# Two expert layers: chunks written out on three engines in place of hardware loops, with a constant expert in the first layer

## The reference

```python
# layer 0: 8 experts, top 2, each expert takes at most 512 rows
slot = where(offset < capacity, expert * capacity + offset, dropped)
h = gelu_tanh(xb[e] @ w1[e]);  y = h @ w2[e]          # xb: (8, 512, 256), w1: 256x1024, w2: 1024x256
out[src] += weight * y
# layer 1: 8 experts, top 2, no capacity
h = gelu(x @ W1[e] + b1[e]);  y = h @ W2[e] + b2[e];  out = sum_e weight[t, e] * y
```

## Time and profile before

| what | value |
|---|---|
| median of 3 runs | 2665.28 us (2664.3 to 2670.51) |
| span of the profiled execution | 2672.0 us |
| PE busy | 2419.7 us, 91% |
| DVE, ACT, POOL busy | 71%, 63%, 68% |
| mean granted clock of PE | 0.972 |
| chunks of layer 0 | about 1507 to 1721 us of the span |
| chunks of layer 1 | about 2340 to 2656 us of the span |

### The profile page before, as it was taken

The page is one execution under the profiler, slowest core; times in us unless marked ns, Lnnn a source line. Parts: engine busy times, 40 slices in busy tenths (PEclk is TensorE's granted clock), DMA queues, the critical chain, the costliest instruction groups (busy, mean ns, idle before and its releaser), DMA issues. The chain is left out here.

```text
span 2672.0 us, 46118 instructions
## 1 busy us (share of the span) xinstructions
PE 2419.7 (91%) x14931; PEld 1416.2 (53%) x15058; DVE 1908.5 (71%) x3499; ACT 1673.2 (63%) x2692; POOL 1804.4 (68%) x1581
## 2 busy tenths in 40 slices
PE   6999999999999999999997588879999999678886
PEld 3555555555555555555553467645444444467665
DVE  7878777787777877777775655468888898764332
ACT  4556756557665566656664555458888788576453
POOL 2677867777777777776768455436878789355553
PEclk9999999999999999999999799989999999699998
DMA  4000000000000000000000744430202020573223
GB/s 144 1 1 1 25 1 1 1 1 5 22 1 1 1 1 1 1 1 1 1 1 15 193 112 116 92 97 18 57 17 58 2 49 1 165 202 72 35 39 60
DMA packets 90917, 107.85 MB, mean 40 GB/s; under 512 B 18867, under 2 KB 80260, under 8 KB 90708
## 3 DMA queue, kind: packets, MB, share of 16 engines
q1 hardware_dynamic: 68500, 80.57, 10.1%
q0 software_dynamic: 21696, 24.98, 6.1%
q10 hardware_dynamic: 544, 0.00, 0.0%
HBM read 68.75 MB, written 25.88 MB: 35 GB/s over the span
## 5 line engine op out<-in xcount | busy, mean ns | idle before, releaser
L417 POOL TENSOR_TENSOR a_acc<-a_acc,a_pf 128x512 f32<-128x512 f32 (+1 forms) x480 | 650.9, 1356 | 312.4 <-ACT a_pf L574 290.7
L574 ACT ACTIVATE a_pf<-a_psS 128x1024 f32<-128x1024 f32 (+1 forms) x288 | 281.5, 977 | 306.1 <-PE a_psS L717 301.8
L869 DVE TENSOR_TENSOR a_pl<-a_pf,a_ph 128x512 f16<-128x512 f32 x448 | 438.2, 988 | 23.2 <-ACT a_ph L580 23.0
L2161 POOL TENSOR_TENSOR c_pl<-c_pf,c_ph 128x512 f16<-128x512 f32 x320 | 374.9, 1199 | 116.9 <-ACT c_ph L2260 116.5
L845 DVE TENSOR_REDUCE a_mx<-a_psA 128x1 f32<-128x512 f32 x504 | 335.3, 683 | 43.7 <-PE a_psA L652 39.6
L580 ACT ACTIVATE a_ph<-a_psS 128x1024 f16<-128x1024 f32 (+1 forms) x288 | 281.5, 977 | 0.0
L1417 POOL DMA_INDIRECT f_sums<-f_xn,f_sidx x78 | 140.5, 1801 | 208.1 <-DVE f_xn L1815 185.6
L1261 DVE TENSOR_TENSOR f_xn<-f_xn 128x256 f16<-128x256 f32 x312 | 130.5, 424 | 197.8 <-ACT f_xn L1230 175.3
L2493 DVE TENSOR_REDUCE c_wf<-c_psA 128x1 f32<-128x512 f32 x384 | 246.5, 681 | 20.1 <-PE c_psA L2332 19.9
L1148 PE MATMUL f_psH<-f_xh,f_w 128*128 128x256 f16 x624 | 173.4, 278 | 83.3 <-ACT f_xn L1230 68.2
L2253 ACT ACTIVATE c_pf<-c_psS 128x1024 f32<-128x1024 f32 x192 | 197.9, 1030 | 67.1 <-PE c_psS L2366 66.0
(11 more groups left out here) (364 smaller groups left out, 6382.0 us busy)
## 6 DMA issues: line engine op xcount, KB each, us to landing
f_stage<-in_L_ffn_w SPq DMA_DIRECT2D x16, 1024.0 KB
f_stage<-in_L_ffn_W SPq DMA_DIRECT2D x16, 1024.0 KB
c_kst<-c_khs SPq DMA_DIRECT2D x64, 100.1 KB, 2.2
a_cx<-in_ctx SPq DMA_DIRECT2D x4, 1536.0 KB
c_cx<-in_ctx SPq DMA_DIRECT2D x12, 512.0 KB, 4.0
f_sums<-X SPq DMA_DIRECT2D x2, 2048.0 KB, 13.2
f_xrow<-f_xn SPq DMA_DIRECT2D x8, 512.0 KB, 4.4
c_kst<-c_kls SPq DMA_DIRECT2D x32, 100.1 KB, 2.2
```

The source lines that it names most:

```text
L417: g.tensor_tensor(acc[0:k, p, :], acc[0:k, p, :], pf[0:k, q % RF, i, :], ALU.add).then_inc(s_acc, 1)
L574: act.activation(pf[0:r, q % RF, 0:k, :], psS[q % 2][0:r, 0:k, :], ACT.Exp, scale=SCALE).then_inc(s_pF, 1)
L869: v.tensor_tensor(pl[0:r, q % RP, i, :], pf[0:r, q % RF, i, :], ph[0:r, q % RP, i, :], ALU.subtract).then_inc(s_pL, 1)
L2161: g.tensor_tensor(pl[0:r, q % RP, i, :], pf[0:r, q % RF, i, :], ph[0:r, q % RP, i, :], ALU.subtract).then_inc(s_pG, 1)
```

## The change

PE, ACT and DVE run their main chunk loops of both layers as Python loops: every iteration is written out as code of its own, with constants where the register m stood. In layer 0 PE takes the chunk's expert from a Python expression ((n + i) * 8 // 16, at most 7) and no longer loads it from `table`, whose iota on POOL goes. In layer 1 PE and DVE still load the expert from `table`, now at a constant place. SP's loop over the experts and the loops of the branch for ties at the kernel's end stay.

```diff
@@ pe_chunk
-            e, e_next = (pe.value_load(experts_of[0:1, bass.ds(c + (0 if last else i), 1)], min_val=0, max_val=E - 1)
-                         for i in range(2))
+            if experts_of is None:
+                e, e_next = (min((n + i) * E // NC, E - 1) for i in range(2))
+            else:
+                e, e_next = (pe.value_load(experts_of[0:1, bass.ds(c + (0 if last else i), 1)], min_val=0, max_val=E - 1)
+                             for i in range(2))
@@ gpsimd
-            else:
-                const(g.iota(table[:, :], pattern=[[1, E], [0, NC // E]], base=0, channel_multiplier=0))
@@ scalar
-                with act.Fori(first_m, last_m) as m:
+                for m in range(first_m, last_m):
                     for p in range(2):
                         act_chunk(act, main, m, p, splits)
@@ tensor
-                with pe.Fori(first_m, last_m) as m:
+                for m in range(first_m, last_m):
                     for p in range(2):
-                        pe_chunk(pe, main, m, p, table, m * 2 + p, splits)
+                        pe_chunk(pe, main, m, p, table if layer else None, m * 2 + p, splits)
...
-                pe_chunk(pe, main, n // 2, n % 2, table, n, False, last=n == NC - 1)
+                pe_chunk(pe, main, n // 2, n % 2, table if layer else None, n, False, last=n == NC - 1)
@@ vector
-                with v.Fori(first_m, last_m) as m:
+                for m in range(first_m, last_m):
                     for p in range(2):
                         dve_chunk(v, main, m, p, take_rows(m, p), splits, prepare_main(m, p))
```

## The result

The changed kernel takes 2624.82 us (median of 4 runs, 2623.94 to 2625.78), the kernel before on the same chip 2664.79 (2663.84 to 2670.51): a ratio of 0.9845, 95% interval 0.9831 to 0.9859. The span of the profiled execution is 2623.2 us, so the two profiles differ by 48.8 us; that of before was of a run some 6 us over its median.

A forecast was written before the change was run, and what follows sets the result against it. PE, busy for 91% of the span, was taken to set the pace. Layer 0 10.3, layer 1 6 and wake-ups 2 made 18.3 us off 2672.0, so 2653.7, scaled by 0.9975 to 2647; range 2632 to 2661.

The forecast's parts named there:

- What bounds the kernel: Expert stages of both layers: PE sets the pace, some 16% idle, nearly all before L1148; idle removed shortens the span.
- Layer 0, PE: Boundaries between layer 0's chunks: loads, branch and computed addresses go, 13.2 us less 2.9 us waiting for DVE, 10.3 us gained.
- The second gap: PE idle before hidden 2 of a chunk, put down to two expert loads and the branch: 13.2 us in layer 0.
- Layer 1, PE: Layer 1's chunk boundaries: the two loads stay, only the branch goes, 0.6 us at ten edges: 6 us, bounds 3 and 7.
- The first gap: PE idle before hidden 0 or 1 of the next chunk, 18.8 us in layer 0, ascribed to gathers; change taken as zero.
- Wake-ups: ACT's 35 ns register operation at loop waits goes: 0.035 to 0.1 us at 33 or so waits, taken as 2 us.
- Instruction streaming: First rival: written-out chunks need about 29 instruction packets, whose fetches could stall PE 35 us, giving 2682; chance 5%.
- The second rival: The gap before hidden 2 is ACT's or reappears elsewhere; only branches and wake-ups count, 3 to 7 us, 2660; chance 13%.
- The third: Rival: PE, less idle, keeps its full clock, about 5 us, and the first gap shrinks by 5: 2636; chance 16%.

The follow-up runs named there:

- merged_early_load_b: Changed kernel with token weights gathered inside the row gathers and, in layer 1, one expert loaded a chunk ahead, on a late-signal chip: 2590.33 us, 0.9693.
- loops_l0_register: Kernel before, loops kept, layer 0's expert from the loop's register instead of the table: 2597.79 us, 0.9994; again on a late-signal chip (_b): 2650.86 us, 0.9950.
- pool_late_l1_b: Changed kernel with three unused additions on POOL before each chunk's gathers in layer 1, on a late-signal chip: 2629.33 us, 0.9870.
- pe_only: Changed kernel with the loops of ACT and DVE put back, PE alone written out with the constant expert: 2646.82 us, 0.9891.
- before_merged_gather_b: Kernel before with token weights gathered inside the row gathers, the two gathers of 32-byte rows gone, on a late-signal chip: 2607.54 us, 0.9741.
- before_again: Kernel before, unchanged, run again for its profile on a chip with late signals: 2676.04 us, 1.0001.
- after_third: Changed kernel, unchanged, on the first chip, where no signal is late: 2590.74 us, 0.9972 of the kernel before.

## Why the prediction was wrong

**What bounds the kernel: right.** PE's idle time before L1148 came off the end: 32.0 - 0.2 - 4.4 = 27.4 us in layer 0 and 13.2 - 1.0 = 12.2 in layer 1 make 39.6 of the 48.8 us between the two spans. Of the rest some 3 us are one chunk of before that ran 17.1 us long beside the stretch at 1.2 GHz; in the chunks of layer 1 after, the granted clock is 1.00. What remains, some 6 us, lies in gaps under 0.2 us and in the first chunks of layer 1, and I haven't split it.

**Layer 0, PE (10.3 us): right in kind and size.** The second gap, 13.2 us, is gone, 4.6 us before L1166 came up, released by DVE L1264 as foreseen, against the 2.9 in the sum. The 0.21 us a chunk is exact where no signal is late at that place (every chunk of merged_early_load_b); here DVE's take starts another 0.1 us late on output 7's signal. The reason given for the gap needs a correction: loads, with the queue emptied before them or with a branch, make it, and a branch without loads makes none (layer 0 of loops_l0_register and of loops_l0_register_b).

**Layer 1, PE (6 us): right in kind.** 20 gaps before hidden 2 of 0.67 us stay, 12.8 us, of the 17.0 before; the branch took 4.2, inside the bounds of 3 to 7. That the queue must first have been emptied is borne out by the first chip, where all terms together are 8 us.

**The first gap (zero, a gain of at most 5): the step that failed.** It was called the gathers' with no mechanism, and therefore put at zero with narrow bounds. It gave all of its 18.8 us in layer 0 and some 9 in layer 1 (47.3 - 17.0 = 30.3 before, 34.1 - 12.8 = 21.3 after). The sentence that "gathers early and late against PE cost alike" was read off one layer in one state, and holds there (pool_late_l1_b confirms it for the other side too), but between the two lies a place where they cost nothing, and the change put layer 0 into it. Which of its edits did so isn't shown by a single run: the loads out leave 11.8 us of the first gap in layer 0, PE alone written out 8.2, everything written out with the loads kept 4.4, all together none. Nothing in the text bounded a gap whose cause was unknown by its own size, which would have been the honest end of the range: 2647 - 19 = 2628 for layer 0 alone, and 2619 with the 9 us of layer 1 that went too.

**Wake-ups (2 us): wrong by the same step.** The register operations at ACT's wait are gone (L1230 of the kernel after has event waits alone), and by pe_only taking ACT and DVE out of their loops is worth 15 us where signals are late. The size of one wake-up was right: ACT's gelu starts some 0.12 us after the record of its matmul in the loops (before_merged_gather_b) and 0.04 us written out (merged_early_load_b). The sum over 33 waits was not. My reading, which no run isolates, is that such tenths decide whether a late signal still holds up hidden 1.

**The rivals.** Instruction streaming did nothing: 11 packets in layer 0, no gap. The second rival is refuted by layer 0. The third came nearest in sign and size, but the clock gave it 3 of 49 us at most, and the mean granted clock of the whole span is 0.972 in both.

## What to carry to other kernels

When an engine waits for another that is itself idle before the awaited instruction, follow one step further back: the end of the matmul record against the start of its waiter tells a late signal from a late engine. A gap whose mechanism isn't known is to be carried in the range with its whole size, for a shift of a few tenths of a microsecond can open or close it. Merge small indirect gathers into rows that are fetched anyway, and compare a kernel on more than one chip before a few per cent are put down to code.

## What the runs showed of the hardware

- Behind two indirect gathers of 128 rows of 32 bytes each, TensorE's completion signals came late in layer 0 of the kernel before, in bunches 76 ns apart; the oldest of a bunch was 1.4 to 3.7 us late (before and before_again), against 0.014 us elsewhere. On one chip, with the same kernel, none did: 2599 us there, in two groups half an hour apart, against 2662 to 2676 on the others. Whether signals of ACT and DVE are held up as well, which part of the way holds them, and in what that chip differs, stays open.
- A loop's branch on PE with two register loads behind it cost about 0.4 us a time where nothing else was late (chunks of 11.30 and 11.68 us in turn); a branch without the loads cost nothing (layer 0 of loops_l0_register). The recorded branch is 0.215 us. The Trainium skill, page "Advanced Engine Details and Errata", section "Control Flow Timing", has about 108 ns for a compare and branch; the rows of this kernel have twice that, and decide.
- Two loads of a register from SBUF, 302 ns each with a step of 151 ns, cost a running PE nothing (layer 1 of after_third) and a PE whose queue had just run dry 0.67 us (layer 1 of the kernel after).
